# Rows scattered straight from the residual stream: routing in batches of six and ten tiles, and double-buffered shared experts, in a decoder layer

## The reference

```python
x = _layernorm(x + _L0_attn_ref(x, ...))            # gated delta rule, 6 heads
x = _layernorm(x + _L0_xattn_ref(x, ctx_512, ...))  # 16 heads, softmax over the 64 context rows
x = _layernorm(x + _L0_ffn_ref(x, ...))

aff = jax.nn.sigmoid(jnp.einsum('bsd,de->bse', x, wa))      # 16 experts
topk_p, topk_i = jax.lax.top_k(aff, 2)
topk_p = topk_p / jnp.sum(topk_p, axis=-1, keepdims=True)
routed = jnp.einsum('bsed,bse->bsd', _experts_all(x, rg, rgb, rw1, rb1, rw2, rb2), combine)
shared = jnp.sum(_experts_all(x, sg, sgb, sw1, sb1, sw2, sb2), axis=2)   # 2 experts
return x + shared + routed
# one expert: (gelu(x @ g + gb) * (x @ w1 + b1)) @ w2 + b2, with g, w1 256x128 and w2 128x256
```

## Time and profile before

| | us |
|---|---|
| median of 3 runs (571.78 to 579.44) | 577.74 |
| profiled execution | 575.09 |
| its span, first to last instruction | 573.3 |
| PE busy in the span | 477.7 (83%) |
| DVE busy | 360.1 (63%) |
| ACT busy | 267.7 (47%) |
| POOL busy | 245.5 (43%) |
| mean granted TensorE clock, share of full | 0.933 |

### The profile page before, as it was taken

The page is one execution under the profiler, slowest core; times in us unless marked ns, Lnnn a source line. Parts: engine busy times, 40 slices in busy tenths (PEclk is TensorE's granted clock), DMA queues, the critical chain, the costliest instruction groups (busy, mean ns, idle before and its releaser), DMA issues.

```text
span 573.3 us, 15410 instructions
## 1 busy us (share of the span) xinstructions
PE 477.7 (83%) x5644; PEld 345.8 (60%) x5644; DVE 360.1 (63%) x794; ACT 267.7 (47%) x673; POOL 245.5 (43%) x335
## 2 busy tenths in 40 slices
PE   5969889578779899999688887776988699999755
PEld 2434344245569799997466665554444478888644
DVE  0759477479967466667567779854741236666536
ACT  2547475525663344455367775644201034444416
POOL 0319021345116675643655453256464015665600
PEclk9979999779799999999899998977989879999969
DMA  8970000016762732003660000012173705554284
GB/s 299 306 219 1 0 0 0 2 42 218 266 126 49 182 109 54 22 3 75 244 260 2 3 2 2 2 61 79 52 222 107 254 19 166 168 171 133 84 291 166
DMA packets 62018, 63.96 MB, mean 112 GB/s; under 512 B 31412, under 2 KB 51964, under 8 KB 61564
## 3 DMA queue, kind: packets, MB, share of 16 engines
q1 hardware_dynamic: 58108, 52.26, 29.3%
q0 software_dynamic: 3840, 10.75, 5.2%
HBM read 37.01 MB, written 28.21 MB: 114 GB/s over the span
## 4 chain that ended last, share of the span: by engine, by line
PE 53%; DVE 27%; issue 8%; ACT 6%; DMA 3%; SPq 1%; another core or an unknown queue 1%; POOL 0%; DVEq 0%; ACTq 0%; POOLq 0%
PE ps L1154 8%; DVE work L1590 5%; PE ps L733 5%; PE ps L1104 4%; PE ps L955 4%; PE ps L1169 3%; PE ps L723 3%; DVE arena L1773 3%; DVE work L1769 3%; PE ps L936 2%; PE ps L1115 2%; PE ps L1145 2%; PE ps L909 2%; PE ps L921 2%; PE ps L887 2%
## 5 line engine op out<-in xcount | busy, mean ns | idle before, releaser
L1590 DVE SCALAR_TENSOR_TENSOR work<-ps,colp,work 96x504 f32<-96x504 f32 (+5 forms) x84 | 59.6, 729 | 22.9 <-ACT work L1225 20.9
L2190 POOL DMA_INDIRECT rows_dr<-work x48 | 46.5, 968 | 60.7 <-DVE work L1967 31.6
L1154 PE MATMUL ps<-vsg,work 128*128 x192 | 51.6, 393 | 0.2 <-ACT work L1524 0.2
L733 PE MATMUL ps<-xT,front 128*96 128x512 f32 (+3 forms) x112 | 50.5, 595 | 0.0
L723 PE MATMUL ps<-front,work 128*128 128x396 f32 x64 | 27.7, 587 | 14.9 <-ACT ab L1218 8.0
L1953 DVE TENSOR_TENSOR work<-ps,xT 128x256 f32<-128x256 f32 x48 | 20.4, 425 | 29.5 <-PE ps L1154 29.1
L2107 POOL TENSOR_TENSOR arena<-front,consts 128x384 f32<-128x384 f32 x32 | 26.5, 830 | 28.8 <-DMA front<-inverse_dr 24.4
L1154 PEld LDWEIGHTS ps<-vsg,work 128*128 128x128 f32 x192 | 34.1, 198 | 3.5 <-issue 0.6
L1530 ACT ACTIVATE work<-work 128x128 f32<-128x128 f32 x48 | 14.8, 309 | 44.2 <-DVE work L1953 37.2
L1104 PE MATMUL ps<-xT,front 128*128 128x512 f32 x64 | 31.5, 650 | 4.5 <-DVE arena L1890 4.5
L733 PEld LDWEIGHTS ps<-xT,front 128*96 128x96 f32 (+1 forms) x112 | 19.0, 176 | 26.0 <-issue 25.6
(11 more groups left out here) (242 smaller groups left out, 1258.7 us busy)
## 6 DMA issues: line engine op xcount, KB each, us to landing
work<-slots_dr SPq DMA_DIRECT2D x48, 136.0 KB
vsg<-wexp_dram SPq DMA_DIRECT2D x4, 1536.0 KB, 12.8
vsg<-rows_dr SPq DMA_DIRECT2D x8, 512.0 KB
blocks_dr<-work SPq DMA_DIRECT2D x16, 192.0 KB, 2.5
mats_dr<-work SPq DMA_DIRECT2D x8, 384.0 KB, 3.2
work<-mats_dr SPq DMA_DIRECT2D x3, 768.0 KB, 5.7
slots_dr<-zero SPq DMA_DIRECT2D x8, 272.0 KB
pads_dr<-zero SPq DMA_DIRECT2D x8, 272.0 KB
```

The lines of the kernel that those rows point to most:

```text
L733: mm = pe.matmul(ps[0:ROWS[j], BANK[j], :], wc3[:, k, CH0[j]:CH0[j] + ROWS[j]], xT3[:, k, bass.ds(g * GT, GT)], start=(k == 0), stop=(k == ...
L1154: mm = pe.matmul(ps[:, 2 + j % 2, 0:2 * F], xgT[:, j % 2, k, :], wres[:, bass.ds(e + k * 2 * F, 2 * F)], start=(k == 0), stop=(k == KD - 1))
L1590: dve.scalar_tensor_tensor(y[:, :, d:T], z[:, :, 0:T - d], taps[0:r, j, KSZ - 1 - d:KSZ - d], y[:, :, d:T], ALU.mult, ALU.add).then_inc(s_ ...
L2190: pool.indirect_dma_start(out=rows_dr, out_offset=bass.IndirectOffsetOnAxis(ap=xg[:, j % XG, S_DEST:S_DEST + 1].bitcast(U32), axis=0), in_ ...
```

## The change

It has these parts.

- A row of `xn` is now 272 columns wide: the 256 of the tile and 16 for tags. The tags (token number, two weights, second expert) are written there by DVE, and the scatter reads `xrow` itself. `stage_rows` on ACT, `staged` and POOL's two tag copies for each tile are gone. Both choices of a token carry the same tags.
- Since a row no longer says which of the two choices it is, DVE works that out slot by slot: `read_tags`, six small instructions for every TG = 4 slots, compares the second expert with the slot's own and writes weight and destination (`wt`, `dest_i`). `weigh_outputs` and POOL's scatter of results read those and wait for them.
- The routing is cut into six and ten tiles in place of eight and eight, and the steps of the first part are spread over turns 9 to 15. Both router exponentials and the tally follow. The second part's steps are split around group 0's products. The second tally now stands behind `shared_hidden(1)` on PE, not ahead of it.
- `ybf` has two buffers. A quarter of `shared_hidden(0)` (two matmuls) goes into turn 16 ahead of `attend_softmax(15)`, another into turn 17. `shared_products(1)` stands behind `place_chosen(1)` and ahead of the routing arithmetic.
- The sums go to a separate `acc`, and `shared_outputs(3)` moves behind `hidden(0)` of the slot loop, `shared_sums(3)` behind `bias_hidden(0)`.
- Around it: the zeroed pads get four tag columns, a few tables move to other places, and start-up has some more small memsets.

The diff, cut to its core (of the routing functions, only the lines that stand after the change):

```diff
-S_WEIGHT = D + 1
+S_TAG = D
+T_TOKEN, T_W0, T_W1, T_E1 = range(4)
 XG, XS, YO, GC, RB = 16, 8, 8, 2, 8
 REG = NTOK + P
-NB2 = NT // 2
+BATCH = [slice(0, 6), slice(6, NT)]
+WIDTH = [b.stop - b.start for b in BATCH]
+TG = 4
...
-        ybf = arena[:, 5120:5120 + 2 * GT].rearrange("p (u c) -> p u c", u=2)
+        ybf = arena[:, 5120:5120 + 4 * GT].rearrange("p (g u c) -> p g u c", g=2, u=2)
+        acc = arena[:, 0:NT * D].rearrange("p (n d) -> p n d", d=D)
...
             def tally_experts(b, bank, c):
 
                 pe.wait_ge(s_mask, at(3 * b + 1))
-                flat = chosen.rearrange("p n e -> p (n e)")
-                pe.matmul(ps[:, bank, c:c + P], consts[:, C_PRE:C_PRE + P], flat, start=True, stop=True)
-                pe.matmul(ps[:, bank, c + P:c + 2 * P], consts[:, C_ONE:C_ONE + P], flat, start=True, stop=True).then_inc(s_pre, 1)
+                flat, w = chosen[b].rearrange("p n e -> p (n e)"), WIDTH[b] * E
+                pe.matmul(ps[:, bank, c:c + w], consts[:, C_PRE:C_PRE + P], flat, start=True, stop=True)
+                pe.matmul(ps[:, bank, c + w:c + 2 * w], consts[:, C_ONE:C_ONE + P], flat, start=True, stop=True).then_inc(s_pre, 1)
+
+            def shared_hidden(g, parts):
+
+                for e, w in parts:
+                    if g == 0 and (e, w) == (0, 0):
+                        pe.wait_ge(s_sub, at(2 * NT))
+                        pe.wait_ge(s_x2e, at(SPG))
+                    if g > 0 and w == 0:
+                        pe.wait_ge(s_yy, at(SH * (g - 1) + e + 1))
+                    for c in range(KD):
+                        o = w * KD * F + c * F
+                        mm = pe.matmul(ps[:, 2 * w + e, :], wsh[:, e, o:o + F], x2T3[:, c, g * GT:(g + 1) * GT],
+                                       start=(c == 0), stop=(c == KD - 1))
+                    if w == 1:
+                        mm.then_inc(s_h, 1)
+
+            all_parts = [(e, w) for e in range(SH) for w in range(2)]
...
+                if i == NT:
+                    shared_hidden(0, all_parts[0:1])
+                if i == NT + 1:
+                    shared_hidden(0, all_parts[1:2])
...
-                        pe.matmul(ps[:, 4 + t, 0:D], ybf[:, e, t * P:(t + 1) * P], wsh[:, e, 2 * KD * F:EW],
+                        pe.matmul(ps[:, 4 + t, 0:D], ybf[:, g % 2, e, t * P:(t + 1) * P], wsh[:, e, 2 * KD * F:EW],
...
-            shared_hidden(0)
+            shared_hidden(0, all_parts[2:4])
+            shared_hidden(1, all_parts)
             tally_experts(1, 6, 0)
-            shared_hidden(1)
...
             pe.wait_ge(s_rt, at(TALLIED[1]))
             pe.wait_ge(s_lt, at(1))
-            for g in range(NG):
+            for g in range(NG - 2):
                 shared_outputs(g)
-                if g + 2 < NG:
-                    shared_hidden(g + 2)
-            pe.wait_ge(s_ac, at(NT))
+                shared_hidden(g + 2, all_parts)
+            shared_outputs(NG - 2)
             pe.wait_ge(s_yy, at(SH * NG))
             pe.wait_ge(s_wr, 64)
             pe.wait_ge(s_slots, at(8))
...
+                if j == 0:
+                    pe.wait_ge(s_ac, at(NT))
...
             hidden(0, which[0])
+            shared_outputs(NG - 1)
             for j in range(NSLOT + 2):
                 if j + 2 < NSLOT:
...
-                act.wait_ge(s_lg, at(NB2 * (b + 1)))
-                act.activation(elog[b].rearrange("p n e -> p (n e)"), logits[:, P * b:P * (b + 1)], ACT.Exp,
-                               scale=-1.0).then_inc(s_el, 1)
-
-            def stage_rows(n):
-
-                act.wait_ge(s_x2, at(n + 1))
-                if n < 5:
-                    act.wait_ge(s_sc, at((2 * SW * (n + 1) - 1) // GT + 1))
-                act.activation(staged(n)[:, :, 0:D], over(x3[:, n, :], 1, 2), ACT.Copy).then_inc(s_xst, 1)
+                act.wait_ge(s_lg, at(BATCH[b].stop))
+                act.activation(elog[b].rearrange("p n e -> p (n e)"), logits[:, E * BATCH[b].start:E * BATCH[b].stop],
+                               ACT.Exp, scale=-1.0).then_inc(s_el, 1)
...
-                if i == NB2 + 2:
+                if i == WIDTH[0] + 2:
                     router_exponentials(0)
-                if i >= 4:
-                    stage_rows(i - 4)
 
             router_exponentials(1)
-            stage_rows(NT - 1)
...
+            def find_best(b, k):
+
+                left = spare[b] if k else elog[b]
+                routed(dve.tensor_reduce(best[:, k, BATCH[b]], left, AXX, ALU.max))
+                routed(dve.tensor_tensor(lower[b], left, over(best[:, k, BATCH[b]], 2, E), ALU.is_lt))
+
+            def mark_best(b, k):
+
+                iota = over(consts[:, C_IOTA:C_IOTA + E], 1, WIDTH[b])
+                index = tags[:, BATCH[b], T_E1] if k else best[:, 2, BATCH[b]]
+                sel = (pick, pick2)[k][:, BATCH[b]]
+                routed(dve.scalar_tensor_tensor(lower[b], lower[b], 64.0, iota, ALU.mult, ALU.add))
+                routed(dve.tensor_reduce(index, lower[b], AXX, ALU.min))
+                routed(dve.tensor_tensor(sel, iota, over(index, 2, E), ALU.is_equal))
+
+            def drop_best(b):
+
+                routed(dve.scalar_tensor_tensor(spare[b], pick[:, BATCH[b]], -4.0, elog[b], ALU.mult, ALU.add))
+
+            def mark_chosen(b):
+
+                dve.tensor_tensor(chosen[b], pick[:, BATCH[b]], pick2[:, BATCH[b]], ALU.add).then_inc(s_mask, 1)
 
             def weigh_chosen(b):
 
+                routed(dve.tensor_tensor(best[:, 3, BATCH[b]], best[:, 0, BATCH[b]], best[:, 1, BATCH[b]], ALU.add))
+                routed(dve.reciprocal(best[:, 4, BATCH[b]], best[:, 3, BATCH[b]]))
+                for k, w in enumerate((T_W0, T_W1)):
+                    dve.tensor_tensor(tags[:, BATCH[b], w], best[:, k, BATCH[b]], best[:, 4, BATCH[b]], ALU.mult).then_inc(s_mask, 1)
+
+            def keep_tally(b, bank, c):
 
                 dve.wait_ge(s_pre, at(b + 1))
+                routed(dve.tensor_copy(counts[b], ps[:, bank, c:c + 2 * WIDTH[b] * E]))
+                assert steps[0] == TALLIED[b], steps
+
+            def count_on(b):
+
+                for m in range(WIDTH[b]):
+                    n = BATCH[b].start + m
+                    routed(dve.tensor_tensor(base[:, n + 1], base[:, n], tally[b][:, m], ALU.add))
 
             def place_chosen(b):
 
+                routed(dve.tensor_tensor(rank[b], rank[b], base[:, BATCH[b]], ALU.add))
                 for k, sel in enumerate((pick, pick2)):
+                    routed(dve.tensor_tensor(lower[b], sel[:, BATCH[b]], rank[b], ALU.mult))
+                    routed(dve.tensor_reduce(best[:, 3, BATCH[b]], lower[b], AXX, ALU.add))
+                    dve.tensor_copy(slots_i[:].rearrange("p (n k) -> p n k", k=2)[:, BATCH[b], k], best[:, 3, BATCH[b]]
                                     ).then_inc(s_slots, 1)
...
+                    keep_tally(0, 0, 2 * P)
                 if 2 <= i <= NT + 1:
                     add_softmax(i - 2)
+                if i == 9:
+                    affinities(0)
+                if i == 10:
+                    find_best(0, 0)
+                    mark_best(0, 0)
                 if i == 11:
+                    drop_best(0)
+                    find_best(0, 1)
                 if i == 12:
+                    mark_best(0, 1)
+                    mark_chosen(0)
+                if i == 13:
                     weigh_chosen(0)
                 if i == 14:
+                    count_on(0)
+                if i == 15:
                     place_chosen(0)
 
             affinities(1)
+            find_best(1, 0)
+            mark_best(1, 0)
+            drop_best(1)
 
             def shared_products(g):
 
                 for e in range(SH):
                     m = SH * g + e
                     dve.wait_ge(s_ge, at(m + 1))
+                    if g > 1:
+                        dve.wait_ge(s_eot, at(SPG * (g - 1)))
+                    dve.scalar_tensor_tensor(ybf[:, g % 2, e, :], ps[:, 2 + e, :], colp[:, E + e + W_B1:E + e + W_B1 + 1],
                                              hbuf[:, e, :], ALU.add, ALU.mult).then_inc(s_yy, 1)
 
             def shared_sums(g):
 
                 for t in range(SPG):
                     n = SPG * g + t
                     dve.wait_ge(s_eot, at(n + 1))
+                    dve.scalar_tensor_tensor(acc[:, n, :], x3[:, n, :], 2.0, ps[:, 4 + t, 0:D], ALU.mult, ALU.add).then_inc(s_ac, 1)
 
             shared_products(0)
+            find_best(1, 1)
+            mark_best(1, 1)
+            mark_chosen(1)
+            weigh_chosen(1)
+            keep_tally(1, 6, 0)
+            count_on(1)
             place_chosen(1)
+            shared_products(1)
             dve.tensor_copy(end_i[:], base[:, NT]).then_inc(s_slots, 1)
...
+            routed(dve.tensor_scalar(expert_g, expert_f, float(E - 1), None, ALU.min))
...
-            for g in range(NG):
-                shared_sums(g)
-                if g + 1 < NG:
-                    shared_products(g + 1)
```

(42 more changed lines are left out.)

149 lines of the change are left out of this document (48 added, 101 removed).

## The result

On record the changed kernel takes 576.74 us (median of 20 runs, 572.77 to 582.96), the kernel before 572.08 beside it: ratio 1.0082, interval 1.0053 to 1.0111. Forecast were 562.4 us and a range of 553 to 571. The profiled execution took 576.92 us (span 575.1), that of before 575.09 (span 573.3). All medians here are of all runs; ratios and intervals leave out slow ones, over 1.5% above the fastest of their kernel.

The account below looks back on a forecast made before the run. The slot loop was taken as bound by matmuls, so the terms sum how far the first turned product moves: -11.5 + 2.4 + 3.2 - 0.7 - 9.2 + 0.5 = -15.3 us, giving 562.4 from the median; range 553 to 571.

Parts of the forecast that it names:

- (b): Loop's tail to the last affinities: two copies gone, two quarters of `shared_hidden(0)` added; net +2.4 us, +1.0 to +4.4.
- (d): Slot numbers to first row load: twenty scatters 1.27 us apart without tag copies, 28.3 us in place of 29.0, -0.7.
- (a): Softmax loop, turns 4 to 15: without the staging copy a turn falls to 5.54 us; gain 11.5, bounds 9.9 and 13.1.
- (c): Last affinities to last slot numbers: ten tiles instead of eight, tally behind `shared_hidden(1)`; 16.6 us, +3.2.
- (e): First row load to first turned product: PE no longer late, `bias_hidden(0)` waits for `b1r`; 15.2 us, -9.2.
- (f): Slot loop: `read_tags` once in four slots mostly hidden in the slack, POOL's added wait free; +0.5 us.
- stop before 378.45: In the old loop DVE stands 2.41 us on an unknown releaser; may vanish or recur, 0 to 1.8 us, half taken, 0.9.
- their 2.6 and 0.9: Loop's tail: cost in us of the first and second quarter of `shared_hidden(0)` placed in the last turns.
- the rival in which DVE holds POOL up: Scatters beside the routing arithmetic can't be issued while it runs; row path grows by 7.8 us: 570, chance 0.05.
- stall by `read_tags`: Rival: `read_tags`, ahead of `bias_hidden`, becomes the slot loop's bound; 578 to 590 us, chance 0.08.
- 3.19 (last start to SP's load): Time in us from the last row scatter's start to SP's first row load, taken over unchanged from before.

Follow-up runs that it names:

- the early broadcast: The kernel after with the bias broadcast `b1r` issued ahead of SP's wait for the scatters: 569.29 us on chip 6; with the pacing too, 557.26 us on chip 0.
- the paced kernel: The kernel after with two one-column GpSimd memsets and a wait ahead of each tile's two scatters: 564.23 us, ratio 0.9855 on chip 3.
- before's burst: The kernel before with all tag copies of a batch done ahead of its scatters, which then start 1.28 to 1.31 us apart: 570.85 us, ratio 1.0007.

## Why the prediction was wrong

The prediction failed in steps (b) and (d), where the two stops fall. The steps, each as the difference of two traces (us, rounded; the last row is in no step):

| step | forecast | on record | chip 12, no stops |
|---|---|---|---|
| (a) loop, turns 4 to 15 | -11.5 | -13.3 | -11.3 |
| (b) to the last affinities | +2.4 | +10.0 | -0.4 |
| (c) to the last slot numbers | +3.2 | +3.2 | +2.3 |
| (d) to the first row load | -0.7 | +5.5 | -0.3 |
| (e) to the first turned product | -9.2 | -8.0 | -4.3 |
| (f) to the end | +0.5 | +3.8 | +3.7 |
| start of turn 4 | 0 | +0.7 | -1.8 |
| spans | -15.3 | +1.8 | -12.0 |

On chips without stops the medians met the sum: before less after is 572.0 - 556.8 = 15.2 us (chip 12), 15.0 and 15.7 (chips 15 and 7); forecast 15.3. That it is so close is partly luck. The pair of traces gives 12.0, after's being of its longest execution there, and the steps are off by up to 4.9 us, some one way and some the other. By its steps, between the two traces of chip 12:

- (a) 74.22 to 62.95: -11.3, forecast -11.5, with the old loop 2.1 shorter than in the earlier trace rows, as its stop before 378.45 is not there. The routing cost 2.0 over eleven free turns, not 3.0.
- (b) 19.11 to 18.76: -0.4, forecast +2.4. Four other traces of after without stops have 17.11, so the forecast was 2.8 to 4.4 too high. What the quarters do cost of their 2.6 and 0.9 was not isolated (above).
- (c) 16.6 us, as forecast, on record too; but the old stretch is 14.3 there, not 13.4, so +2.3.
- (d) 28.97 to 28.65: -0.3, forecast -0.7. Scatters (424.66 - 400.23) / 19 = 1.29 apart, forecast 1.27, beside all the routing arithmetic: the rival in which DVE holds POOL up is wrong, on record too (413.05 to 437.53).
- (e) 21.68 to 17.42: -4.3, forecast -9.2. The path is the forecast one: PE stands 5.53 us ahead of the first L1152 on the DMA (forecast 5.4), then the product waits for the bias broadcast. The new stretch took 14.6 to 16.7 in five other traces without stops, against the forecast 15.2. More than half of the miss is the old end, 24.42 on record: there the matmuls of `shared_outputs(3)` took 5.41 us, on chip 12 3.72 (granted clock 0.72 from 450.62 to 456.66 on record, and 1.00 from 449.56 to 453.92 on chip 12).
- (f) No stall by `read_tags` is seen. But PE stands idle 5.92 us ahead of the first turned product and starts the slots at half clock (0.50 from 445.26 to 450.00 on chip 12, and from 462.95 to 467.69 on record), where before had 0.90 and 0.93 in its first 4.74 us. From the product to the end of the span it is 112.2 us in both traces of after, 108.4 and 108.5 in before: a cost of 3.7 that the sum did not have. Where PE stood only 0.2 us ahead of the product, with the early broadcast, it is 109.1 and 109.2 at clock 1.00:

```profile
440.22:445.26 5.04, 0.00 (x1) 0.01 (x1) 2.00 (x7) 0.58 (x2) 0.00 (x0) 0.90 0.44 157
445.26:450.00 4.74, 4.74 (x13) 3.90 (x14) 1.96 (x10) 1.49 (x6) 0.00 (x0) 0.50 0.00 0
```

On record and on chip 6 two terms of the prediction failed. One is in (d) the sentence "By the rows the scatters cost nothing more than their 1.27". The scatters kept their pitch, 1.29 on record, but what was beside them did not: (b) took 29.60 us, of which the first stop is 10.8, and in (d) the "3.19 (last start to SP's load)" became 8.98, since SP waits for its pad stores. The other is in (a) the stop before 378.45, bounded as "0 to 1.8 us". I had seen a packet of the instruction queue fall into that stop and took it for the cause. Its other neighbour was POOL's first scatter, at 376.37. On a chip of the other kind a packet of that queue passes between 376 and 377 as well, and DVE's wait is 0.94 us with a known releaser, not 2.41 with an unknown one. (The Trainium skill, "Runtime: NRT & Kernel Launch", instruction fetch mechanics, calls such a crossing mostly hidden; on chip 12 the trace agrees, with 0.94 us.) The stop was probably a small case of what after has twice: an engine waits long past its producer's end while scatters are issued. I priced it as noise of one place and gave it no rival of its own; with twelve and twenty scatters in a row it came to 10.8 and 5.9 us, the latter by way of SP's stores: DVE's wait of 18.38 us beside them cost nothing more that can be seen, for row load to product took 16.44 us with it and 17.42 without. Why the engines stop stays open.

What is shown: the same program stops on one chip or session and not on another; where it does, the stops eat the whole gain; and they lie beside the rows' scatters only. What is argued: that spacing matters. For it, on record before's pairs 3.3 us apart cost 2 us, and SP's pads took 11.4 as they did on chip 12; after's rows without gaps cost 17, and the pads took 29.0. Against it, a burst without gaps is harmless on the other chips, and the slot loop's scatters, 1.6 apart, show no stop on either kind (112.2 us from the product to the end on both). That the scatters read the loop's own rows, where before's read a staged copy, is a rival that no run on a chip with stops has tested either. A run of the paced kernel on such a chip would test the first, before's burst there the second; both are missing.

## What to carry to other kernels

A wait whose releaser the profile does not know is a rival with a price, not half a term: look at all that began just before it, on every queue, and ask what the change makes more of. Before explaining a difference, run the unchanged kernel again, on another chip; here that alone was worth 16 to 20 us, and the time of the kernel before didn't show it. A match of the sum is no proof of its steps: compare them one by one, in traces of one chip. And a part that shortens one path (rows loaded 5.2 us sooner in before brought 1.0) pays only with a part that shortens the other; here that is argued to be the double buffer, which was not undone by itself.

## What was unexpected of the hardware

Of six chips on which it can be told (0, 3, 6, 7, 12, 15), one gives this kernel 573.0 us and the others 555 to 558 (on chip 0 it ran only paced, 562.6 us), while the kernel before takes about 572 on both kinds (567.3 once, on chip 0); the kind shows in the missing landing times of its traces. It is one chip and the record's, whose number is not known, so whether it is the chip or the session that makes it is open. There SP's sixteen pad stores take 28.8 to 29.0 us beside the scatters against 12.0 to 12.8. And two hundred empty instructions in TensorE's program left no instruction in the trace (15459 with and without) and did not change its time (558.12 us against 557.6).
